# RMS inverses of a fused conditioned block: square sums turned and added up by VectorE, the inverses spread through a DRAM row

## The reference, cut to what matters

```python
# stage 0: layer norm, then a per-sequence shift
out = (x - mean) * rsqrt(var + 1e-5) * weight + bias
out = (out + tanh(cond @ lin_w.T + lin_b)) * weight + bias
# stage 1: attention and a gated feed-forward part, each behind an adaptive RMS norm
def ada_rmsnorm(x, t, gamma_w, beta_w):
    return (t @ gamma_w.T) * (x * rsqrt(mean(x * x, axis=-1) + 1e-6)) + (t @ beta_w.T)
x = x + (t @ attn_alpha_w.T) * attention(ada_rmsnorm(x, t, attn_...))   # 16 heads of 16
x = x + (t @ ffn_alpha_w.T) * swiglu(ada_rmsnorm(x, t, ffn_...))        # 256 -> 1024 -> 256
```

## Time and profile before

| | |
|---|---|
| median of the runs | 1029.57 us |
| the profiled execution | 1028.54 us |
| its span, first to last instruction | 1026.7 us |
| PE busy | 986.7 us (96%) |
| PE weight loads busy | 923.9 us (90%) |
| DVE busy | 668.0 us (65%) |
| ACT busy | 624.8 us (61%) |
| POOL busy | 565.1 us (55%) |
| moved by DMA | 23.37 MB, mean 23 GB/s |

### The profile page before, as it was taken

The page is one execution under the profiler, slowest core; times in us unless marked ns, Lnnn a source line. Parts: engine busy times, 40 slices in busy tenths (PEclk is TensorE's granted clock), DMA queues, the critical chain, the costliest instruction groups (busy, mean ns, idle before and its releaser), DMA issues.

```text
span 1026.7 us, 28723 instructions
## 1 busy us (share of the span) xinstructions
PE 986.7 (96%) x11292; PEld 923.9 (90%) x11292; DVE 668.0 (65%) x1311; ACT 624.8 (61%) x1775; POOL 565.1 (55%) x532
## 2 busy tenths in 40 slices
PE   5677999999999999999999999999999999999997
PEld 5566999999999999999999999999999999998897
DVE  5566666666666666666666666666666666666554
ACT  4566565666666666666666666666666666666432
POOL 4476646565474656547465654746565474443320
PEclk9788999999999999999999999999999999999999
DMA  6100001000100100010000001000000000000000
GB/s 206 43 21 22 2 11 33 11 23 12 32 12 11 33 11 23 11 33 12 12 33 12 23 11 34 11 12 33 12 23 12 12 12 12 12 11 13 11 12 21
DMA packets 20917, 23.37 MB, mean 23 GB/s; under 512 B 1200, under 2 KB 20272, under 8 KB 20784
## 3 DMA queue, kind: packets, MB, share of 16 engines
q1 hardware_dynamic: 20784, 21.54, 6.6%
HBM read 13.15 MB, written 8.39 MB: 21 GB/s over the span
## 4 chain that ended last, share of the span: by engine, by line
PE 85%; issue 5%; DVE 4%; ACT 4%; POOL 2%; DMA 0%; POOLq 0%; SPq 0%; ACTq 0%; DVEq 0%
PE psum L280 17%; PE psum L282 16%; PE psum L281 16%; PE psum L474 5%; PE psum L473 5%; PE psum L472 5%; PE psum L408 5%; PE psum L397 4%; PE psum L419 4%; PE psum L331 2%; PE psum L318 2%; ACT probs L822 2%; PE psum L310 1%; PE psum L323 1%; DVE least L584 1%
## 5 line engine op out<-in xcount | busy, mean ns | idle before, releaser
L280 PE MATMUL psum<-xf_hi,ffn_hi 128*128 128x256 f32 x1024 | 288.3, 282 | 2.8 <-DVE normed_f L629 1.6
L281 PE MATMUL psum<-xf_lo,ffn_hi 128*128 128x256 f32 x1024 | 286.4, 280 | 0.0
L282 PE MATMUL psum<-xf_hi,ffn_lo 128*128 128x256 f32 x1024 | 285.5, 279 | 0.0
L822 ACT ACTIVATE probs<-psum,least 128x64 f32<-128x64 f32 x976 | 212.1, 329 | 53.5 <-DVE least L584 30.1
L652 DVE SCALAR_TENSOR_TENSOR late<-tanh,psum 128x512 f32<-128x512 f32 x128 | 88.0, 688 | 223.7 <-ACT tanh L845 223.7
L1002 POOL TENSOR_TENSOR probs<-probs,inv_sum 128x512 f32<-128x512 f32 x128 | 139.5, 1090 | 108.3 <-DVE inv_sum L605 107.9
L280 PEld LDWEIGHTS psum<-xf_hi,ffn_hi 128*128 128x128 f32 x1024 | 192.8, 188 | 3.7 <-issue 3.7
L851 ACT ACTIVATE prod_hi<-late 128x512 fp32r<-128x512 f32 x128 | 80.7, 631 | 187.9 <-DVE late L660 185.7
L281 PEld LDWEIGHTS psum<-xf_lo,ffn_hi 128*128 128x128 f32 x1024 | 193.1, 189 | 0.0
L282 PEld LDWEIGHTS psum<-xf_hi,ffn_lo 128*128 128x128 f32 x1024 | 192.7, 188 | 0.0
L474 PE MATMUL psum<-prod_hi,ffn_lo 128*128 128x256 f32 x512 | 143.2, 280 | 0.0
(11 more groups left out here) (102 smaller groups left out, 2246.8 us busy)
## 6 DMA issues: line engine op xcount, KB each, us to landing
out_t_dram<-x_res SPq DMA_DIRECT2D x32, 256.0 KB, 2.1
xin<-x_dram SPq DMA_DIRECT2D x15, 512.0 KB, 3.8
w_raw<-attn_w_dram SPq DMA_DIRECT2D x1, 1024.0 KB, 7.1
x_res<-gate_w_dram SPq DMA_DIRECT2D x1, 1024.0 KB, 9.9
late<-hidden_w_dram SPq DMA_DIRECT2D x1, 1024.0 KB, 11.9
x_res<-out_w_dram SPq DMA_DIRECT2D x1, 1024.0 KB, 5.5
xin<-x_dram SPq DMA_DIRECT2D x2, 256.0 KB, 3.0
k_heads<-mod_w_dram SPq DMA_DIRECT2D x1, 320.0 KB, 5.0
```

The costliest lines, as they stand in the source:

```text
L280: pe.matmul(out, stat_hi, mov_hi, start=first, stop=False)
L281: pe.matmul(out, stat_hi, mov_lo, start=False, stop=False)
L282: return pe.matmul(out, stat_lo, mov_hi, start=False, stop=last)
L822: op = act.activation(probs[g % 2][:, h * SEQ:(h + 1) * SEQ], scores[:, h // 2, h % 2], ACT.Exp, bias=least[g % 2][:, h:h + 1], scale=-1.0)
```

## The change

PE no longer makes means. `turn_squares` transposes the square sums into `norm_bank`, 128 columns for 128 tokens, and DVE adds up each run of 128 columns (a `tensor_reduce` from PSUM with 512 elements in each partition in a full group) and then adds epsilon in a second instruction. The factor 1/256 moves into ACT's squares as a scale of 1/16 ahead of the squaring. For groups from 0 on, PE no longer spreads the inverses. SP waits for POOL's power, stores the four columns to a row in DRAM (one of two rows in turn), waits for the store and reads the row back to all 128 partitions (2 KB each, 256 KB in a full group) into the space of `w_raw`, and DVE multiplies from there. The token order inside the turned columns is chosen so that each partition holds two neighbouring tokens (`token_cols`). The attention parts 0 and 1 (groups -2 and -1) still use PE's spread. `hidden` waits in slot 1 for the new reduction (`ms_read`) and in slot 2, from group 0 on, for nothing of the norm.

```diff
--- before.py
+++ after.py
@@ -48,6 +48,7 @@
 NC = 4
 VW = 2 * DH
 SCALE = (HEADS / D) ** 0.5
+ROOT_D = D ** -0.5
 LN_EPS, RMS_EPS = 1e-5, 1e-6
 
 SHIFT, A_GAMMA, A_BETA, A_ALPHA, F_GAMMA, F_BETA, F_ALPHA = range(7)
@@ -85,7 +86,7 @@
         vecs = sb("vecs", [P, 4, KT])
         w_sq = sb("w_sq", [P, KT])
         ident = sb("ident", [P, P])
-        mean_col = sb("mean_col", [P, 1])
+        warm = sb("warm", [P, 2])
         minus_half = sb("minus_half", [P, TILES])
         mask = sb("mask", [P, 4])
         pair = sb("pair", [P, 2])
@@ -105,6 +106,7 @@
 
         squares_a = sb("squares_a", [P, KT, PART])
         square_sum_a = sb("square_sum_a", [P, PART])
+        square_mean = sb("square_mean", [P, 4])
         mean_sq = sb("mean_sq", [P, 4])
         normed_a = sb("normed_a", [P, KT, PART])
         xn_hi = sb("xn_hi", [P, KT, PART], F32R)
@@ -132,6 +134,8 @@
         prod_hi = [sb(f"prod_hi{i}", [P, 3 * PART], F32R) for i in range(2)]
         prod_lo = [sb(f"prod_lo{i}", [P, BLK], F32R) for i in range(2)]
 
+        inv_dram = nc.dram_tensor("inv_dram", [2, 2 * PART], F32).ap()
+        inverse = [w_raw[:, i * 2 * PART:(i + 1) * 2 * PART] for i in range(2)]
         gated_f = late[:, 0:KT * PART].rearrange("p (k c) -> p k c", k=KT)
         prod, act_gate = late[:, 2 * BLK:3 * BLK], late[:, 3 * BLK:4 * BLK]
         ffn_raw = [x_res[:, 3:5].rearrange("p b k c -> p (b k c)"), late[:]]
@@ -151,7 +155,8 @@
         stats_made, merged, var_made, rstd_made = sem("stats_made"), sem("merged"), sem("var_made"), sem("rstd_made")
         x_normed, x_turned, res_made = sem("x_normed"), sem("x_turned"), sem("res_made")
         squared_a, sq_sum_a, squared_f, sq_sum_f = sem("squared_a"), sem("sq_sum_a"), sem("squared_f"), sem("sq_sum_f")
-        ms_mm, ms_out, inv_made, inv_spread = sem("ms_mm"), sem("ms_out"), sem("inv_made"), sem("inv_spread")
+        ms_mm, ms_read, ms_out = sem("ms_mm"), sem("ms_read"), sem("ms_out")
+        inv_made, inv_spread = sem("inv_made"), sem("inv_spread")
         gamma_a, scaled_a, xn_a = sem("gamma_a"), sem("scaled_a"), sem("xn_a")
         hi_a, lo_a = sem("hi_a"), sem("lo_a")
         k_mm, k_out, q_mm, q_out, v_mm, v_out = (sem("k_mm"), sem("k_out"), sem("q_mm"), sem("q_out"),
@@ -168,6 +173,8 @@
         prod_made, prod_hi_made, prod_lo_made = sem("prod_made"), sem("prod_hi_made"), sem("prod_lo_made")
         out_mm, gated_f_made, y_made = sem("out_mm"), sem("gated_f_made"), sem("y_made")
 
+        inv_stored, spread_loaded = sem("inv_stored"), sem("spread_loaded")
+
         block = ctx.enter_context(nc.Block())
 
         def is_part(m):
@@ -190,6 +197,9 @@
 
         def norm_cols(grp, n):
             return slice(0 if is_part(grp + 2) else 2 * n, 4 * n if is_part(grp - 2) else 2 * n)
+
+        def token_cols(grp, ap, i):
+            return ap[:].rearrange("p (t i) -> p i t", i=2)[:, i] if grp >= 0 else ap[:, i * P:(i + 1) * P]
 
         def part_mod(row, m):
             return mod[:, row, :, m * PSEQ:(m + 1) * PSEQ].unsqueeze(3).broadcast_to([P, KT, PSEQ, SEQ])
@@ -240,6 +250,22 @@
             def load_mod(first, last, signal):
                 sp.dma_start(mod_stage[:, first * D:last * D].rearrange("p (w d) -> p w d", d=D),
                              mod_w[first:last].rearrange("w c d -> c w d")).then_inc(signal, 16)
+
+            def spread_inverses(grp):
+                which = slice(0 if is_part(grp + 2) else 1, 2 if is_part(grp - 2) else 1)
+                sp.wait_ge(inv_made, grp + 3)
+                sp.dma_start(inv_dram[grp % 2].rearrange("(w p i) -> p w i", w=2, i=2)[:, which],
+                             mean_sq[:].rearrange("p (w i) -> p w i", i=2)[:, which]).then_inc(inv_stored, 16)
+                if grp <= 1:
+                    sp.wait_ge(w_lo_made, 4)
+                else:
+                    sp.wait_ge(scaled_a, min(grp + 1, NPART))
+                if grp >= 4:
+                    sp.wait_ge(scaled_f, grp - 3)
+                sp.wait_ge(inv_stored, 16 * (grp + 1))
+                cols = slice(which.start * PART, which.stop * PART)
+                sp.dma_start(inverse[grp % 2][:, cols], inv_dram[grp % 2:grp % 2 + 1, cols].partition_broadcast(P)
+                             ).then_inc(spread_loaded, 16)
 
             def store(m):
                 sp.wait_ge(y_made, m + 1)
@@ -268,6 +294,8 @@
                 if (s + 4) % (2 * PSEQ) == 0 and (s + 4) // (2 * PSEQ) + 2 < NBLK:
                     sp.wait_ge(x_turned, (s + 4) // PSEQ + 2)
                     load_x((s + 4) // (2 * PSEQ) + 2)
+                if s % PSEQ == 1 and s >= 0 and is_group(s // PSEQ):
+                    spread_inverses(s // PSEQ)
                 m = (s - FFN_AT - PSEQ - 1) // PSEQ
                 if (s - FFN_AT - 1) % PSEQ == 0 and is_part(m):
                     store(m)
@@ -292,11 +320,9 @@
                 if j == 0 and is_part(grp + 2):
                     pe.wait_ge(res_made, 2 * (grp + 2) + 2)
                 if j == 1 and is_group(grp):
-                    pe.wait_ge(ms_out, grp + 3)
-                if j == 2 and is_part(grp + 2):
+                    pe.wait_ge(ms_read, grp + 3)
+                if j == 2 and grp < 0:
                     pe.wait_ge(scaled_a, grp + 3)
-                if j == 2 and is_part(grp - 2):
-                    pe.wait_ge(scaled_f, grp - 1)
 
             def norm_bank_free(s):
                 norm_bank_read(norm_step(s - 1), (s - 1) // PSEQ)
@@ -311,23 +337,20 @@
                                           xin[m // 2 % 2][:, m % 2 * 2 + i, kt * P:(kt + 1) * P], ident[:])
                 mm.then_inc(x_turned, 1)
 
-            def mean_squares(grp):
+            def turn_squares(grp):
                 if is_part(grp + 2):
                     pe.wait_ge(sq_sum_a, grp + 3)
                     for i in range(2):
-                        mm = pe.matmul(norm_bank[:, i:i + 1], square_sum_a[:, i * P:(i + 1) * P], mean_col[:],
-                                       start=True, stop=True)
+                        mm = pe.transpose(norm_bank[:, i * P:(i + 1) * P], token_cols(grp, square_sum_a, i), ident[:])
                 if is_part(grp - 2):
                     pe.wait_ge(sq_sum_f, grp - 1)
                     for i in range(2):
-                        mm = pe.matmul(norm_bank[:, 2 + i:3 + i], square_sum_f[:, i * P:(i + 1) * P], mean_col[:],
-                                       start=True, stop=True)
+                        mm = pe.transpose(norm_bank[:, (2 + i) * P:(3 + i) * P], token_cols(grp, square_sum_f, i), ident[:])
                 mm.then_inc(ms_mm, 1)
 
             def spread_inverses(grp):
                 pe.wait_ge(inv_made, grp + 3)
-                cols = norm_cols(grp, 1)
-                for i in range(cols.start, cols.stop):
+                for i in range(2):
                     mm = pe.transpose(norm_bank[:, i * P:(i + 1) * P], mean_sq[:, i:i + 1].broadcast_to([P, P]),
                                       ident[:])
                 mm.then_inc(inv_spread, 1)
@@ -492,11 +515,11 @@
                 if j == 0 and is_part(grp + 2):
                     turn_x(grp + 2)
                 if norm_step(s) == 1 and is_group(grp) and s >= 0:
-                    mean_squares(grp)
-                if norm_step(s) == 2 and is_group(grp) and s >= -4:
+                    turn_squares(grp)
+                if norm_step(s) == 2 and -4 <= s < 0:
                     spread_inverses(grp)
                 if s == FIRST_SLOT + 1:
-                    mean_squares(grp)
+                    turn_squares(grp)
                 if s == FIRST_SLOT + 2:
                     spread_inverses(grp)
                 if s == FIRST_SLOT + 1:
@@ -620,25 +643,33 @@
 
             def mean_squares_out(grp):
                 dve.wait_ge(ms_mm, grp + 3)
-                if grp >= -1:
+                if grp >= 1:
+                    dve.wait_ge(inv_stored, 16 * grp)
+                elif grp >= -1:
                     dve.wait_ge(inv_spread, grp + 2)
                 cols = norm_cols(grp, 1)
-                dve.tensor_scalar(mean_sq[:, cols], norm_bank[:, cols], RMS_EPS, None, ALU.add).then_inc(ms_out, 1)
-
-            def scale_by_rms(normed, first):
-                return dve.tensor_tensor(normed[:], normed[:],
-                                         norm_bank[:, first:first + PART].unsqueeze(1).broadcast_to([P, KT, PART]),
+                dve.tensor_reduce(square_mean[:, cols], norm_bank.rearrange("p (n c) -> p n c", c=P)[:, cols], AX_X, ALU.add
+                                  ).then_inc(ms_read, 1)
+                dve.wait_ge(ms_read, grp + 3)
+                dve.tensor_scalar(mean_sq[:, cols], square_mean[:, cols], RMS_EPS, None, ALU.add).then_inc(ms_out, 1)
+
+            def scale_by_rms(normed, inverses):
+                return dve.tensor_tensor(normed[:], normed[:], inverses.unsqueeze(1).broadcast_to([P, KT, PART]),
                                          ALU.mult)
 
             def scale_a(m):
```

(20 more changed lines are left out.)

## The result

The changed kernel takes 1083.39 us (median of 4 runs, 1079.65 to 1084.24) against 1028.93 us: ratio 1.0529, 95% interval [1.0509, 1.0549]. It is 54 us slower, where I had forecast 1006 us; that is outside the range. What came about is rival 2: the round trip of the inverses (store, load and the two starts, R) is longer than what is free. The profiled execution took 1079.65 us (span 1077.7), the shortest of the four.

A forecast was written before the change was run, and what follows sets the result against it. PE bounds groups 3 to 29 at 29.98 us. From 1028.54 us: 23.9 less (26 x 0.92), 1.4 and 1.3 less at start and end, 2.9 more at the start, 1 to 2 more for tight slots: about 1006, range 1001 to 1024.

The forecast's parts named there:

- rival 2: Round trip of the inverses exceeds 5.64 us, so DVE and PE wait; at 6.0 about 1042 us; chance 0.10.
- What PE gives up: Four transposes replace four N=1 matmuls in slot 1, slot 2's transposes go: group 29.98 to 29.06 us, 0.92 less.
- rival 3: PE gains less: strided operand costs a second pass, about 1018 us, or DVE-ACT ring holds, about 1012; chance 0.15.
- What DVE gets: In slot 1 a reduction adds 0.7 us, covered by existing waits; multiplications by the inverses from SBUF cost no more.
- The loop: Reduction, power, store, load, multiplication and back to the reduction: 24.33 us plus round trip, of which 4.73 is free.
- the size of R: Round trip of the inverses: store 1.7, load 2.6, two starts 0.1 each, 4.5 us, between 3.6 and 5.4.
- rival 1: Round trip of 4.8 to 5.5 us becomes the bound, leaving some gain; at 5.2 about 1019 us; chance 0.18.
- The start: Groups 0 to 2 can't hide the round trip, 2.9 us more; groups 2 and 3 gain 1.4 on PE.
- The end: Last four groups have half the norm: 1.8 us less, of which 0.5 is given back for the last.

The follow-up runs named there:

- experiment 3: Changed kernel, but PE spreads the inverses as before, without the added store and load, and square sums are turned without a stride: 1016.07 us.
- experiment 2: Changed kernel, but from group 3 on the load reads the row stored by the group before, so it doesn't wait for its own store: 1016.58 us.
- experiments 8: Changed kernel with the row stored in 16-byte runs and the load reading 128 separate rows of attention weights instead of one row: 1025.98 us.
- experiment 7: Changed kernel with the row in DRAM laid out so that each partition stores one 16-byte run instead of two of 8 bytes: 1042.41 us.
- experiment 6: Changed kernel with the store of the four columns made twice, one behind the other, each waited for: 1263.98 us, one run.
- experiment 5: Changed kernel, but PE spreads the inverses as before in groups 0 to 3, with the row in DRAM from group 4 on: 1080.65 us.
- experiment 9: Changed kernel with the row in DRAM only in groups 4 to 30 and attended_lo ahead of the two multiplications in slot 2: 1009.06 us.

## Why the prediction was wrong

- *What PE gives up*: right in kind, and four fifths of it in size. 0.92 us a group were forecast, 29.98 to 29.06; where the round trip is hidden, the group takes 29.25, a gain of 0.73. Slot 1 is 7.57 with unstrided square sums (experiment 3) and 7.66 with strided ones: the stride costs 0.09, not the 0.5 that I kept as a bound. The weight loads do take longer, which I had named as the sign of rival 3, but they cost a sixth of what it said. Slots 2 and 3 are 7.07 and 7.06 instead of 7.00 and 7.01; why, no run shows.
- *What DVE gets*: right. The reduction is covered (PE is busy throughout slot 1 in experiment 2), L657 from SBUF takes 0.69 us.
- *The loop*: right in form. By it R is free to 4.73 us, and above that the group is 24.33 + R. With the average R of each run the sum gives 29.7, 30.1, 31.4 and 35.6 for experiments 8, 7, the changed kernel and 6. Measured, with the slots at the lower clock put back to 7.1, are 29.7, 30.0, 31.1 and 35.0: the sum is a little high, the more so the longer R.
- **The step that failed is the size of R**: "R = 4.5, between 3.6 and 5.4". Measured is 7.1, and the two terms share the miss. The store was taken as 1.7 us, with an upper end of 2.2 from a 4 KB *load*, and took 3.0. There were no rows of stores in small runs; I said so in rival 2, but let the load's row bound the sum. The load was taken as 2.6, with an upper end of 3.0 from a load of separate rows, and took 3.9. That all partitions read the same 2 KB I named in rival 1 and gave no number. Both bounds came from transfers of another shape. The estimate by the Trainium skill's figure for a DMA's fixed part ("DMA: Bandwidth & Descriptors", section "Anatomy of one DMA"), R = 4.8, was nearly as far off. The Trainium skill's remark on the same page, section "Specifications", that transfers under 512 B are made by reading, changing and writing back, pointed the right way; but no run here shows that this is the cause, and the stores in 16-byte runs, which are under 512 B too, mostly landed after 1.4 us.
- *Rival 2* had the mechanism and the break-even (5.64), with a chance of 0.10. At R = 7.08 its terms give 26 x 1.43 = 37.2 us more. Measured are 40.4 for these 26 groups, of which 9.1 are the clock: the closeness of 37 and 40 is partly luck.
- *The start*: forecast 1.5 us worse (2.9 lost, 1.4 gained), measured 8.6. In group 1 L657 came at 72.72 us against 67.04, 5.7 us late where I had 2.0: 2.1 more by the longer R (6.6 in that group), and 1.5 because the power there (POOL) already began at 65.39 us instead of 63.85. With PE's spread there (experiment 5) the start is 1.8 us better than before.
- *Left out*: the clock. Six slots at a lower clock are 9 us in the profiled execution (mean granted clock 0.970; in the other three 0.967 to 0.973).
- *The end*: 2.7 us worse instead of 1.3 better. It is the wait for the row there too: without it (experiment 2) the end takes 105.4 us, with PE's spread (experiment 9) 106.2, as before.

## What to carry to other kernels

Price a transfer by a row of its own shape: direction, length of one run, and whether the readers share an address. A bound from a transfer of another shape is no bound; where none is in the trace, the case in which it is much dearer deserves a large chance. When a latency is put into a loop between engines, write down the loop's length and the latency that is free, then look at what is queued behind the waiting instruction: here one swap of two calls was worth 60 us, without touching the latency. And TensorE as the bound engine, when it is made to wait, can pay twice, by the wait and by its clock.

## What the runs showed of the hardware that was not expected

- A 2 KB store to DRAM in runs of 8 bytes landed after 3.0 us, in runs of 16 bytes mostly after 1.4. Issued 0.5 us behind a 256 KB store they took 4.0 and 3.0, and 2 KB from SBUF to SBUF took 1.8.
- 128 partitions reading one 2 KB row: 3.8 to 3.9 us; 128 rows of 2 KB: 2.8 to 3.2; one row of 512 B: 3.6.
- Weight loads with a stride of two fp32 elements took longer: 209 against 143 ns. PE's groups in the changed kernel (strided), then in experiment 3 (not):

```profile
L348 PEld LDWEIGHTS psum<-ident,square_sum_f 128*128 128x128 f32 x64 | 10.5, 209 | 0.4 <-issue 0.3
```

```profile
L330 PEld LDWEIGHTS psum<-ident,square_sum_f 128*128 128x128 f32 x64 | 8.0, 143 | 0.4 <-issue 0.3
```

- Idle time of PE at the end of slot 2 was now and then followed by a stretch at 1.2 GHz in slot 3. Ahead of the six such slots of the changed kernel it was 1.7 to 2.1 us, ahead of the nine of experiment 5 1.6 to 3.2, and ahead of all 27 of experiment 6 4.7 to 6.6. But gaps of the same length, up to 2.2 and 2.8 us in the first two, were not followed by one; what decides stays open. In experiment 7, with gaps of at most 1.4 us, the clock stayed at 1.00 in the steady part.
